# Sorting a graph layer's edges in four parts instead of two

## The reference

```python
# x (8192, 512); src, dst (131072,) with dst ascending; edge_weight (131072,)
h   = layernorm(x) @ W.T                                   # L0_gnn, W is 512 x 512
x   = x + segment_sum(edge_weight[:, None] * h[dst], src)  # out row = src, gathered row = dst
x   = x + ffn(layernorm(x))                                # 7 small layers on a few features of marked rows
```

## Time and profile before

| | us |
|---|---|
| median of 3 runs | 2067.34 (2066.86 to 2069.97) |
| the profiled execution | 2060.78 |
| its span, first to last instruction | 2059.0 |
| h products, first to last matmul of L1048 | 22.6 to 298.3 |
| walk, first to last matmul of L1123 | 356.1 to 1889.1 |

### The profile page before, as it was taken

How to read it: one execution, slowest core, us unless ns; L and a number is a source line. 1 busy time by engine, 2 the same in 40 slices (tenths; PEclk the granted TensorE clock), 3 DMA queues, 4 the chain that set the end, 5 groups by cost and what they waited for, 6 DMA issues and landing times.

```text
span 2059.0 us, 26013 instructions
## 1 busy us (share of the span) xinstructions
PE 1610.9 (78%) x3844; PEld 667.1 (32%) x3845; DVE 1074.5 (52%) x3132; ACT 460.9 (22%) x1104; POOL 1070.5 (52%) x1114
## 2 busy tenths in 40 slices
PE   5899982787877887887777778778778777876796
PEld 3455541233332333333223222223223222322442
DVE  9588887886777777863222222222222222223554
ACT  5677620010001001100100111211211211211341
POOL 1000001566666666666666666666666666664930
PEclk9999995899999999899998989999999999998796
DMA  9211111566666666666666666666666666664323
GB/s 359 95 67 62 67 57 42 152 170 180 174 177 177 176 177 172 177 175 178 179 174 175 183 174 180 174 174 179 179 174 180 178 174 179 176 176 119 113 96 120
DMA packets 120880, 323.70 MB, mean 157 GB/s; under 512 B 20338, under 2 KB 37522, under 8 KB 120722
## 3 DMA queue, kind: packets, MB, share of 16 engines
q0 software_dynamic: 81920, 268.50, 45.9%
q1 hardware_dynamic: 38802, 53.48, 7.2%
HBM read 288.35 MB, written 33.55 MB: 156 GB/s over the span
## 4 chain that ended last, share of the span: by engine, by line
PE 60%; issue 18%; SPq 11%; DVE 8%; DVEq 1%; ACT 1%; DMA 0%; another core or an unknown queue 0%; ACTq 0%
PE psum L1123 43%; PE psum L1048 9%; SPq L416 4%; PE psum L1211 4%; SPq L326 2%; SPq L427 2%; SPq L380 2%; DVE region L859 2%; PE psum L1037 1%; DVE region L775 1%; DVEq L859 1%; PE psum L1058 1%; PE psum L1064 1%; DVE region L779 1%; DVE region L765 1%
## 5 line engine op out<-in xcount | busy, mean ns | idle before, releaser
L479 POOL DMA_INDIRECT region<-h_rows,region x1024 | 990.4, 967 | 885.4 <-DVE region L795 332.3
L1123 PE MATMUL psum<-region 128*128 (+1 forms) x2300 | 1187.4, 659 | 332.4 <-issue 169.2
L859 DVE SCALAR_TENSOR_TENSOR region<-region 128x128 f32 (+1 forms) x1150 | 399.7, 349 | 780.2 <-PE psum L1123 431.6
L1123 PEld LDWEIGHTS psum<-region 128*128 128x128 f32 x2300 | 441.0, 206 | 1065.4 <-issue 1055.6
L1048 PE MATMUL psum<-region 128*128 128x512 f32 x512 | 233.5, 600 | 15.0 <-ACT region L548 15.0
L627 ACT ACTIVATE x<-psum 128x512 f32<-128x512 f32 x64 | 38.2, 597 | 730.4 <-PE psum L1123 514.9
L629 ACT ACTIVATE x<-psum 128x512 f32<-128x512 f32 x64 | 38.2, 597 | 613.6 <-PE psum L1123 405.5
L775 DVE COPY_PREDICATED region<-region 128x256 f32<-128x256 int32 x258 | 137.9, 535 | 0.0
L1048 PEld LDWEIGHTS psum<-region 128*128 128x128 f32 x512 | 93.6, 193 | 109.8 <-issue 94.1
L765 DVE TENSOR_TENSOR region<-region 128x256 int32<-128x256 f32 x258 | 108.1, 419 | 19.9 <-ACT region L564 18.7
L777 DVE TENSOR_TENSOR region<-region 128x256 f32<-128x256 f32 x258 | 111.0, 430 | 0.6 <-DVE region L775 0.6
(11 more groups left out here) (152 smaller groups left out, 701.8 us busy)
## 6 DMA issues: line engine op xcount, KB each, us to landing
x<-in_x SPq DMA_DIRECT2D x16, 1024.0 KB, 14.4
h_rows<-region SPq DMA_DIRECT2D x64, 256.0 KB, 2.0
region<-h_rows,region POOLq DMA_INDIRECT x1024
out<-x SPq DMA_DIRECT2D x4, 2816.0 KB, 10.7
out<-x SPq DMA_DIRECT2D x8, 640.0 KB, 3.4
region<-in_L_gnn_weight SPq DMA_DIRECT2D x1, 1024.0 KB, 7.6
region<-in_src SPq DMA_DIRECT2D x2, 256.0 KB, 7.9
region<-in_dst SPq DMA_DIRECT2D x2, 256.0 KB, 6.5
```

The source lines that it names most:

```text
L479: pool.indirect_dma_start(gathered[:, (c + 1) % RING, :], None, h_dram, bass.IndirectOffsetOnAxis(ap=dst_i[g][:, i:i + 1], axis=0),).then_ ...
L859: dve.scalar_tensor_tensor(spread[:, slot % SR, :], iota_n[:, bass.ds((tile - (g * T + 1)) * P, P)], src_f[g][:, bass.ds(chunk - (g * NC + ...
L1123: pe.matmul(psum[:, bass.ds(tile % AGG * D, D)], spread[:, slot % SR, :], region[:, bass.ds(chunk % RING * D, D)], start=False, stop=True, ...
```

## The change

Edges are cut in PARTS = 4 parts of 32,768. NC falls to 256 and QB to 15; a compare step works on 128x128, and a part has 113 compare steps and 15 turns of four transposes instead of eight. The staircase of a part has 256 + 64 - 1 = 319 steps, so there are 1276 steps in all, and still 1024 chunks. Part 0 and the first HEAD slots of part 1 are planned beside the h products; each later part is sorted beside the walk of the part ahead. `slots_with_steps` spreads the slots evenly over the steps of a walk, all but the last 12. By its arithmetic HEAD is 41 slots (17 compare steps), and a walk takes 347, 388 and 388 slots over 307 steps, up to three behind a step. A slot "rest" counts half there, so that from "turn" to "turned" there are 3.5 steps.

All tables now stand on row 32g. The kept weights lie in SBUF for every part (before, in PSUM for the second). `build` loads only the tile of a step and works the chunk out. DVE waits for the last h product before the walk.

```diff
-    HALVES = 2
-    NC = E // (P * HALVES)
+    PARTS = 4
+    NC = E // (P * PARTS)
...
+    LAST_STEPS = 12
...
-        pack, flip, key_step, weight_step, turn, turned, tile = 9.0, 0.4, 1.05, 1.0, 1.3, 2.7, 3.75
+        vector_times = {"pack": 6.0, "flip": 0.3, "keys": 0.6, "weights": 0.85, "turned": 1.9, "maxima": 2.5,
+                        "counts": 2.0, "rows": 2.0, "index": 0.4, "source": 0.8}
+        turn, tile, start = 0.9, 3.75, 24.0
...
+        end = start + T * tile + turn * (TURNS + 3)
+        head, is_open = 0, False
+        for g in range(2):
+            for at, (what, _, _) in enumerate(SORT_SLOTS):
+                if g and vector > end - 12.0 and not is_open:
+                    head = at
+                    break
...
+    def slots_with_steps(g):
+
+        left = SORT_SLOTS[HEAD if g == 0 else 0:] if g + 1 < PARTS else []
+        share = {"keys": 1.0, "weights": 1.0, "turned": 1.2, "flip": 0.4, "rest": 0.5}
+        room = (NS - LAST_STEPS) / max(1.0, sum(share.get(what, 0.7) for what, _, _ in left))
+        found, at = [0] * NS, 0.0
+        for what, _, _ in left:
+            found[int(at * room)] += 1
+            at += share.get(what, 0.7)
+        return found
...
-            load_edges(1)
+            for g in range(1, PARTS):
+                load_edges(g)
...
-                        kept = single(low_kept if g == 0 else bank(LOW_BANK)[:, 0:NC // 2], j)
+                        kept = single(low_kept, j)
...
-                        if g == 0:
-                            dve.wait_ge(s_key_in[g], turns)
-                        else:
+                        if turns > (TURNS, HEAD_TURNS, 0, 0)[g]:
                             dve.wait_ge(s_turn_k[g], turns)
-                            dve.tensor_copy(keys[now], bank(KEY_BANK)).then_inc(s_key_in[g], 1)
+                            dve.tensor_copy(keys[now], turned_keys).then_inc(s_key_in[g], 1)
...
-            for what, ready in zip(sort_edges(0), INVERTS):
+            second = sort_edges(1)
+            for what, ready in zip(chain(sort_edges(0), islice(second, HEAD)), INVERTS):
...
-                    dve.reg_load(walk, stair[row_of(g), i:i + AHEAD, :].rearrange("p i w -> p (i w)"))
-                tile, chunk = placed(dve, walk, g, i)
+                    dve.reg_load(walk, stair[row_of(g), i:i + AHEAD, 0])
...
-            second = sort_edges(1)
-            for i in range(NS):
-                build(0, i)
-                next(second, None)
...
-            for _ in second:
-                pass
-            for i in range(NS):
-                build(1, i)
+            dve.wait_ge(s_mm, T)
+            for g in range(PARTS):
+                following = second if g == 0 else sort_edges(g + 1)
+                for i, slots in enumerate(slots_with_steps(g)):
+                    build(g, i)
+                    for _ in range(slots):
+                        next(following)
...
-            for i in range(NS):
-                add_step(1, i)
+            for g in range(PARTS):
+                following = islice(SORT_SLOTS, HEAD if g == 0 else 0, None)
+                for i, slots in enumerate(slots_with_steps(g)):
+                    add_step(g, i)
+                    for what, _, _ in islice(following, slots):
+                        of_sort(g + 1, what)
```

More of the change, by code:

```diff
@@ L1 @@
 from contextlib import ExitStack
+from itertools import chain, islice
 import concourse.bass as bass
@@ L93, in gnn_ffn @@
     TURNS = 2 * (QB - 7) - 1
-    assert sum(what == "turn" for what, _, _ in sort_slots()) == TURNS
+    SORT_SLOTS = list(sort_slots())
+    ON_TENSOR = ("turn", "maxima summed", "counts summed", "rows summed")
+    assert sum(what == "turn" for what, _, _ in SORT_SLOTS) == TURNS
     def plan():
-        pack, flip, key_step, weight_step, turn, turned, tile = 9.0, 0.4, 1.05, 1.0, 1.3, 2.7, 3.75
[L100 to L111, removed]
-        inverts[-1] += LOADS - b
-        return behind, inverts
@@ new lines, in plan @@
+        inverts[-1] += LOADS - b
+        return behind, inverts, head
+    BEHIND_TILE, INVERTS, HEAD = plan()
+    HEAD_TURNS = sum(what == "turn" for what, _, _ in SORT_SLOTS[:HEAD])
+    def slots_with_steps(g):
[7 more added lines that the diff above has]
+        return found
@@ L347, in progress @@
             steps = turns = buffer = 0
-            for what, _, _ in sort_slots():
+            for what, _, _ in SORT_SLOTS:
                 if what == "turn":
@@ L596, in _ @@
                     h_rows_out(n - 1)
-                    for turn in range(TURNS):
-                        if TURN_TILE[turn] == n - 1:
-                            turn_out(turn)
+                    turns_out(n - 1)
                 some_statistics(3)
             h_rows_out(T - 1)
-            for turn in range(TURNS):
-                if TURN_TILE[turn] == T - 1:
-                    turn_out(turn)
+            turns_out(T - 1)
             def seed(u):
@@ L616, in _ @@
                 seed(u)
-            for u in range(HALVES * T):
+            for u in range(PARTS * T):
                 g, n = divmod(u, T)
@@ L724, in single @@
                     return a.rearrange("p (b d) -> p b d", d=1 << (j if j < 7 else j - 7))
-                for what, k, j in sort_slots():
+                for what, k, j in SORT_SLOTS:
                     if what == "pack":
@@ L1100, in _ @@
                 multiply(n)
-                for turn in range(TURNS):
-                    if TURN_TILE[turn] == n:
-                        turn_edges(0, turn)
-            turn_maxima(0)
-            sum_counts(0)
-            sum_rows(0)
+                for tile, g, what in BEHIND_TILE:
+                    if tile == n:
+                        of_sort(g, what)
             walk = counters(pe, *[f"pe_stair{k}" for k in range(2 * AHEAD)])
@@ L1125, in add_step @@
                           start=False, stop=True, skip_group_check=True).then_inc(s_done, 1)
-            turns = 0
-            second = sort_slots()
-            for i in range(NS):
-                add_step(0, i)
-                what = next(second, ("", 0, 0))[0]
-                if what == "turn":
-                    turn_edges(1, turns)
-                    turns += 1
-                elif what == "maxima summed":
-                    turn_maxima(1)
-                elif what == "counts summed":
-                    sum_counts(1)
-                elif what == "rows summed":
-                    sum_rows(1)
-            assert turns == TURNS and next(second, None) is None
-            for i in range(NS):
-                add_step(1, i)
+            for g in range(PARTS):
[4 more added lines that the diff above has]
+                        of_sort(g + 1, what)
+            assert turned == [TURNS] * PARTS
             go, = counters(pe, "pe_live")
```

150 lines of the change are left out of this document (92 added, 58 removed).

## The result

The changed kernel takes 2209.97 us (median; 2202.95 to 2217.1), the kernel before 2067.1 us beside it. The ratio is 1.071, with a 95% interval of 1.068 to 1.074: 7% slower, where 2037 us were forecast. The profiled execution took 2208.2 us, its span is 2206.4 us.

What follows compares the result with a forecast made beforehand. PE bounds the h products, DVE the 57 us before the walk, a cycle of slow SP, full ring and slow clock the walk. -55 - 5 + 30 = -30 us gives 2031 us profiled, 2037 us median; 8 in 10: 1998 to 2137 us.

Steps and rivals of the forecast that it cites:

- The start: Start of the walk after the last h product: 301 us in place of 356, term -55 us.
- The cover up to the last product: Part 0's sort and HEAD, done by 248 us, hide under the h products ending at 294 us.
- The 126 added steps: Walk: more steps with chunks still 1024; pace per chunk stays, but low-clock stretches, turns and seams cost +30 us.
- the terms -5 and +30: Walk: -5 us for a better PE clock at its beginning, +30 us for 126 steps more.
- Rival 1: Walk: every added step is paid at PE's price, +130 us, 2137 us in all; chance 0.25.
- The change part by part: Section pricing h products, part 0, walk's start, 126 steps more, sorts beside walks and kept weights; sum -30 us.
- The sorts beside the walks: Parts' sorts during walks: DVE needs 265 us of a 383 us walk, so hidden behind PE and SP.
- What would show it: Wrong if gathers reach 1.6 us, PE waits over 45 us more for builds, or POOL's mean issue passes 1.1 us.
- rival 2: Walk: turns too close, PE misses 1 us at each of 43 turns, +45 us, 2082 us; chance 0.12.
- Rival 3: Walk: DVE's SBUF copies of kept weights block POOL's gathers, put at +25 us, 2062 us; chance 0.08.
- The third alarm: Walk: POOL's mean issue passing 1.1 us would show DVE's copies blocking POOL.

Runs made afterwards that it cites:

- four_old_build: Changed kernel with the old build (load of 16 neighbouring registers, tile and chunk, no arithmetic): 2041.6 us, ratio 0.989 to the kernel before.
- four_old_build_again: Changed kernel with the old build, run once more beside the changed kernel itself: 2044.9 us, ratio 0.990 to the kernel before.
- two_extra_matmuls: Kernel before with 64 more step-sized products in the second walk, into a bank nobody reads: 2063.2 us, ratio 0.998.
- four_kept_in_psum: Changed kernel with the old build and the kept weights in PSUM beside the walks: 2024.9 us, ratio 0.987 to the kernel before.
- four_old_build_5: Changed kernel with the old build, repeated in another group of runs: 2020.5 us, ratio 0.989 to the kernel before.
- four_offsets: Changed kernel with build loading finished offsets from a table, no arithmetic, three register instructions a build: 2022.8 us, ratio 0.988 to the kernel before.
- four_load_of_16: Changed kernel with the old load of 16 neighbouring registers, chunk still worked out: 2162.1 us, ratio 1.056 to the kernel before.
- four_as_changed: The changed kernel itself, run once more beside the same kernel with the old build: 2221.4 us, ratio 1.075 to the kernel before.

## Why the prediction was wrong, point by point

- **The start** was right. Product end 295.8 us (forecast 294), first step 303.2 (301): -53 us for the -55 us of the sum. The way there wasn't: part 0's tables were written at 243 us, not 221, and the last compare step of HEAD began at 266.5 us, not at 247. The operations at 128x128 take about 290, 236 and 349 ns, where the working from the earlier trace rows gives 295, 216 and 405, so the 22 us aren't in them. They are in the turns: DVE sat idle for 67 us waiting for ACT's copies at part 0's 15 turns, 4.5 us each, where the sum had 2.9 us a turn. The cover up to the last product swallowed them.
- **The 126 added steps** were right in kind and near in size: with the terms -5 and +30 the walk grows by 25 us; with the old build it grew by 35 us in the profile of four_old_build (1568 against 1533) and by 46 in that of four_old_build_again. In the first PE was busy for 83 us more in the walk and idle for 52 less (281 of the 332; the prediction had 100 less). two_extra_matmuls shows the same without the rest. Rival 1 was wrong.
- **The failed step is one that isn't there.** "The change part by part" has no term for the edit of `build`, which the description of the change names. It was taken as a simplification, less to load. It is worth 176 us (2221.4 - 2044.9 in one group), all of the loss and more; in the kernel with two parts, 103 us (2169.4 - 2066.2). By the queue's instructions: three a build became five, because "the chunk worked out" is instructions; and the load of eight tiles two words apart takes 1.83 us where the 16 neighbouring words took 1.10 us.
- **"The sorts beside the walks"** gave DVE a share of 0.69 to 0.74, from busy time and 0.25 us a build beyond the overlap, and called that hidden. The queue was in use 0.82 of the time with the sort already before the change, as the table shows, and 0.86 with four parts and the old build: small instructions and loads, 69 and 57 us of a part of 766, were missing from the share. The miss alone cost nothing that shows: four parts with the old build are 1% faster. With the edit on top it decided: 0.96.
- **What would show it.** Two of the three alarms went off, 1.69 us a gather (rival 1's) and 126 us more of PE waiting for builds (rival 2's, 162.2 less 35.9), and neither rival was the cause. With the turns as close and the old build PE waits for builds for 63.9 us in the whole walk of four_old_build and for 55.6 in that of four_old_build_again, 28 and 20 us more than before, so that turns 3.5 steps apart don't cost the 45 us of rival 2. No run changed the distance of the turns alone. The third alarm stayed silent (960 ns).
- **Rival 3**, after the Trainium skill's "SBUF — State Buffer", section "SBUF: two separate sides", asked whether float32 copies from SBUF to SBUF hold up POOL's descriptors. The runs don't show it: four_kept_in_psum, without those copies beside the walks, and four_old_build_5, with them, give 0.987 and 0.989, with overlapping intervals, and POOL's mean issue is 964 and 969 ns.
- **The forecast holds for the kernel without that edit**, which takes 2041.6 us where 2037 were forecast, but the match is in part luck: the walk's growth of 35 to 46 us in place of 25 is set off in part by the tail after it, 7 us shorter (162 against 169 us), which the sum left as it was.

Open are two things. Whether the number of register instructions or their kind does the harm: four_offsets (three) and four_load_of_16 (five) differ in both, and the two attempts to add instructions alone left three a build. And what makes the stretches of 0.7 us. Of 78 on SP in the profile before (three or more instructions of 0.7 us, at most 4 us apart) 53 began 4 to 8 us after POOL's last pause, while POOL issued back to back; but its pauses, those over 0.6 us, are themselves about 8 us apart (median), and no kernel showed that this is the cause. The loading of the program's code comes to mind as well: the chip without stretches loaded as much (107 and 52 packets against 106 and 52), so the amount alone doesn't make them.

## What to carry to other kernels

Cost a loop by its queue too, not by its engine's busy time alone: add every register instruction and load of one iteration, look how much of it lies under engine work, and compare the sum with the loop's pace. A large change that also touches a small helper of the inner loop has two changes in it; time the small one alone. Here the kernel with the four parts and the old build is the one to keep: 0.989 of the time before, in three groups (0.989, 0.989, 0.990).

## What was not expected of the hardware

- A load of 8 registers from words two apart held DVE's queue 1.83 us; one of 16 registers from neighbouring words 1.10 us. More data in order was cheaper than half of it with a stride.
- In four of the five groups, each on a chip of its own, small instructions of SP's, DVE's and PE's queues lasted about 0.7 us each, in stretches, instead of 0.04 to 0.1; which queue had more of them followed the kernel: 396 on SP, 211 of PE's register instructions and 67 on DVE in four_old_build_again, 283, 36 and 248 in four_as_changed. On one chip there were none, and the kernel before took 1837 us instead of 2066.
- A register move or an addition in the source is not always an instruction: two constant moves vanished, two dependent operations became 23 ns more in one instruction, while the subtraction that works out a chunk came to two instructions more.
